# An opening reordered on five queues: GpSimd takes the subtraction for S4, the two weight groups of block 0 are split ahead of S3 and S4, and Bd's table is loaded earlier

## The reference

```
x = x + einsum('bct,bcd->bdt', x, W0[subject])
x = x + einsum('bct,bcd->bdt', x, W1[adapter])
x = x + einsum('bct,bcd->bdt', x, W2[adapter]) + fside[adapter][:, :, None]
gate = x @ Wg + (x @ Ag[adapter]) @ Bg[adapter]     # 512 -> 2048
up   = x @ Wu + (x @ Au[adapter]) @ Bu[adapter]     # 512 -> 2048
h    = silu(gate) * up
x = x + h @ Wd + (h @ Ad[adapter]) @ Bd[adapter]    # 2048 -> 512
```

## Time and profile before

| | us |
|---|---|
| median of 3 runs | 1249.04 |
| lowest, highest | 1248.89, 1249.17 |
| the profiled execution's own time | 1250.41 |
| its span, first to last instruction | 1248.4 |
| granted TensorE clock, mean | 1.000 |

### The profile page before, as it was taken

How to read it: one execution, slowest core, us unless ns; L and a number is a source line. 1 busy time by engine, 2 the same in 40 slices (tenths; PEclk the granted TensorE clock), 3 DMA queues, 4 the chain that set the end, 5 groups by cost and what they waited for, 6 DMA issues and landing times.

```text
span 1248.4 us, 17946 instructions
## 1 busy us (share of the span) xinstructions
PE 1236.3 (99%) x6222; PEld 1035.2 (83%) x6222; DVE 957.7 (77%) x1536; ACT 551.7 (44%) x987; POOL 710.7 (57%) x597
## 2 busy tenths in 40 slices
PE   8999999999999999999999999999999999999998
PEld 6888888888888888888888888888888888888887
DVE  6987777887778777788678768777867877677775
ACT  3744454444444354454334444444433443443432
POOL 4476556558745556546864556555676554444453
PEclk9999999999999999999999999999999999999999
DMA  5956455544896345445398535535559742323433
GB/s 186 308 193 212 119 143 147 160 137 136 310 316 216 107 129 147 129 145 171 119 373 297 168 101 152 152 120 155 146 186 359 251 118 78 95 82 102 118 87 116
DMA packets 142199, 211.68 MB, mean 170 GB/s; under 512 B 44192, under 2 KB 88480, under 8 KB 142112
## 3 DMA queue, kind: packets, MB, share of 16 engines
q1 hardware_dynamic: 117696, 135.45, 34.1%
q0 software_dynamic: 23552, 73.95, 19.2%
q10 hardware_dynamic: 864, 1.15, 0.3%
HBM read 166.46 MB, written 44.04 MB: 169 GB/s over the span
## 4 chain that ended last, share of the span: by engine, by line
PE 93%; DVE 4%; DMA 1%; issue 1%; ACT 1%; another core or an unknown queue 0%; SPq 0%; DVEq 0%; ACTq 0%
PE pd L1680 28%; PE px L1680 28%; PE py L1680 14%; PE pz L1680 7%; PE pz L1697 3%; PE pv L1726 2%; PE pv L1724 2%; PE pd L1986 2%; PE py L1697 2%; PE px L1697 2%; PE pd L1823 1%; PE pd L1707 1%; PE py L1805 1%; PE px L1805 0%; DVE wg_lo L1325 0%
## 5 line engine op out<-in xcount | busy, mean ns | idle before, releaser
L758 POOL TENSOR_TENSOR h_lo<-g,h_hi 128x512 fp32r<-128x512 f32 x127 | 182.8, 1439 | 288.0 <-ACT h_hi L898 285.6
L722 POOL DMA_INDIRECT b_got<-b_table,idx_b x192 | 197.8, 1030 | 59.0 <-issue 49.7
L1457 DVE TENSOR_TENSOR acc<-pd,acc 128x512 f32<-128x512 f32 x252 | 167.3, 684 | 55.1 <-PE pd L1680 50.9
L1680 PE MATMUL px<-xo_hi,wg_hi 128*128 128x512 f32 x516 | 207.2, 402 | 1.9 <-ACT up L898 0.6
L1325 DVE TENSOR_TENSOR wg_lo<-w_raw,wg_hi 128x512 fp32r<-128x512 f32 (+1 forms) x256 | 182.2, 716 | 32.7 <-issue 19.7
L1680 PE MATMUL pd<-wd_hi,h_hi 128*128 128x512 f32 x512 | 202.8, 396 | 0.0
L1680 PE MATMUL px<-xo_hi,wg_lo 128*128 128x512 f32 x516 | 202.4, 392 | 0.0
L1680 PE MATMUL pd<-wd_lo,h_hi 128*128 128x512 f32 x512 | 201.0, 393 | 0.0
L1680 PE MATMUL px<-xo_lo,wg_hi 128*128 128x512 f32 x516 | 200.9, 389 | 0.0
L1680 PE MATMUL pd<-wd_hi,h_lo 128*128 128x512 f32 x512 | 199.8, 390 | 0.0
L898 ACT ACTIVATE wg_hi<-w_raw 128x512 fp32r<-128x512 f32 (+1 forms) x260 | 146.3, 570 | 117.1 <-PE py L1697 73.9
(11 more groups left out here) (317 smaller groups left out, 2439.2 us busy)
## 6 DMA issues: line engine op xcount, KB each, us to landing
w_raw<-w_gu SPq DMA_DIRECT2D x65, 512.0 KB
wd_raw<-w_dn SPq DMA_DIRECT2D x64, 256.0 KB
xo_hi<-xops SPq DMA_DIRECT2D x21, 512.0 KB, 6.1
xo_lo<-xops SPq DMA_DIRECT2D x21, 512.0 KB, 7.4
acc<-x SPq DMA_DIRECT2D x8, 1024.0 KB, 8.7
ad_raw<-ad_table SPq DMA_DIRECT2D x16, 512.0 KB
xops<-st_hi SPq DMA_DIRECT2D x24, 256.0 KB, 2.8
xops<-st_lo SPq DMA_DIRECT2D x24, 256.0 KB, 2.9
```

Source lines behind the costliest of these rows:

```text
L722: gp.indirect_dma_start(out=dst, out_offset=None, in_=rows_of, in_offset=bass.IndirectOffsetOnAxis(ap=rows.bitcast(U32), axis=0)).then_inc ...
L758: return gp.tensor_tensor(dst, src_raw, src_hi, ALU.subtract)
L1457: ins = dve.tensor_tensor(dst, pd[j][:, :], dst, ALU.add)
L1680: ins = pe.matmul(psum, w_parts[wi], x_parts[xi], start=(start and i == 0), stop=(stop and i == 2), skip_group_check=more)
```

## The change

On five queues instructions are moved; none is added, and one changes its engine.

- SP: the load of `bd_rows` goes ahead of `store_ad(0, 0)`, `store_b(0)` and `load_b(1)`.
- POOL: Bd's subtraction comes after two of three gathers instead of after `b_low(1)`; the subtraction for S4 is POOL's now, after the six gathers of `b_got` and ahead of `gather_ad(0, 1..3)`.
- ACT: Bd's copy goes ahead of `b_high(1)`; the four `weights_high(1, g)` and the last two `ua_high` go ahead of `sum_high(S3)` and `sum_high(S4)`, with `keep_s1(1)` between; `weights_high(2, 1)` goes behind `keep_c21`; in block 1 of each quarter the second `down_high` goes behind `keep_s2`.
- DVE: `weights_low(1, 2)` and `(1, 3)` go ahead of `ua_low(0, 1, 0)`, `o_low(S3)` ahead of `select(0, 0)`, `o_low(S4)` is gone; in block 0 of the first quarter `select` and `c12` come ahead of `sums(2)` and `weights_low(2, 0)`; `half_numbers` goes from the start of block 1 to its end, ahead of `add_down`.
- PE: in block 0 of the first quarter `lora(pz, b, 0, 0)` comes after `S3` instead of before it.

```diff
@@ SP @@
             load_weights(1)
+            sp.wait_ge(pick_mm, 2)
+            sp.dma_start(bd_raw()[0], bd_rows).then_inc(bd_in, 16)
             store_ad(0, 0)
             store_b(0)
             load_b(1)
-            sp.wait_ge(pick_mm, 2)
-            sp.dma_start(bd_raw()[0], bd_rows).then_inc(bd_in, 16)
             load_ad(0, 0)
@@ POOL @@
-            gather_b(0, 0, 0)
-            b_low(1)
+            gather_b(0, 0, 0, range(2))
             gp.wait_ge(bd_hi_done, 1)
             low(bd_raw()[2], bd_raw()[0], bd_raw()[1]).then_inc(bd_done, 1)
+            b_low(1)
+            gather_b(0, 0, 0, range(2, CHUNKS))
             gather_b(0, 0, 1)
             gp.wait_ge(o_done, LOW_ORDER.index(S1) + 1)
             gp.wait_ge(o_s3_sum, TP)
+            gp.wait_ge(o_hi, HIGH_ORDER.index(S4) + 1)
+            gp.wait_ge(o_done, LOW_ORDER.index(S3) + 1)
+            low(xo_lo[:, S4, :], s_raw[S4], xo_hi[:, S4, :]).then_inc(o_done, 1)
             for g in range(1, AD_GROUPS):
                 gather_ad(0, g)
@@ ACT @@
             ua_high(0, 0, 1)
-            b_high(1)
             act.wait_ge(bd_in, 16)
             copy(bd_raw()[1], bd_raw()[0]).then_inc(bd_hi_done, 1)
-            sum_high(S3, o_s3_sum)
-            sum_high(S4, o_s4_sum)
+            b_high(1)
...
             ua_high(0, 1, 1)
+            keep_s1(1)
+            sum_high(S3, o_s3_sum)
+            sum_high(S4, o_s4_sum)
...
-                if b != 1:
+                if b != 1 and n > 1:
                     keep_s1(k)
...
                 keep_s5(k)
-                if b == 1:
-                    down_high(q * BLOCKS + 1)
...
                 keep_s2(k)
+                if b == 1:
+                    down_high(q * BLOCKS + 1)
...
                 if n == 1:
                     weights_high(n + 1, 0)
-                    weights_high(n + 1, 1)
...
                 if (q, b) == (0, 0):
                     keep_c21()
+                    weights_high(n + 1, 1)
@@ DVE @@
             o_low(S2, s_raw[S2])
-            ua_low(0, 1, 0)
             weights_low(1, 2)
             weights_low(1, 3)
+            ua_low(0, 1, 0)
+            o_low(S3, s_raw[S3])
             select(0, 0)
-            o_low(S3, s_raw[S3])
             ua_low(0, 1, 1)
-            o_low(S4, s_raw[S4])
...
                     u3(k)
+                    select(q, 1)
+                    c12(k)
                     if not q:
                         sums(n + 1)
-                    select(q, 1)
-                    if not q:
                         weights_low(n + 1, 0)
-                    c12(k)
...
-                if n == 2:
-                    half_numbers()
...
+                if n == 2:
+                    half_numbers()
                 for phase_at in down_phases(q, b):
@@ PE @@
                 product(pz, A12, True, True)
-                ... lora(pz, b, 0, 0).then_inc(p2_mm, 1)
+                if n > 1:
+                    lora11()
...
                 product(px, S3, False, True).then_inc(p7_mm, 1)
+                if n == 1:
+                    lora11()
```

More of the change, by code:

```diff
@@ L1972, in _, with lora11 @@
                 product(pz, A12, True, True)
-                pe.wait_ge(b_got_in[0], (q * SUPER + b // 2 + 1) * CHUNKS * 16)
-                pe.wait_ge(u_done, 6 * q + 3)
-                lora(pz, b, 0, 0).then_inc(p2_mm, 1)
+                def lora11():
+                    pe.wait_ge(b_got_in[0], (q * SUPER + b // 2 + 1) * CHUNKS * 16)
+                    pe.wait_ge(u_done, 6 * q + 3)
+                    lora(pz, b, 0, 0).then_inc(p2_mm, 1)
+                if n > 1:
+                    lora11()
                 pe.wait_ge(w_done[2], n + 1)
```

## The result

| | before | changed |
|---|---|---|
| median of 15 executions, us | 1249.17 | 1251.58 |
| lowest, highest | 1247.80, 1250.83 | 1249.19, 1256.61 |
| the profiled execution, own time | 1250.41 | 1251.75 |
| its span | 1248.4 | 1249.7 |
| granted TensorE clock, mean | 1.000 | 0.998 |

The account below looks back on a forecast made before the run. PE's own work was taken to set the time, leaving only its few pauses to gain. A gain of 1.9 us less 0.3 for `half_numbers` gave -1.6: median 1249.04 to 1247.4 us, range 1246.2 to 1249.2.

Parts of the forecast that it names:

- opening and block 0: Block 0: S3 starts at 49.62 on PE, S4 at 52.8; POOL's S4 subtraction takes 2.39 us and costs nothing.
- new wait for group 0 ahead of block 1: Block 1's start: PE waits 0.75 us for DVE's group 0, so A11 starts at 57.45, a gain of 0.75.
- block 1: Block 1 on PE: S3 at 63.4, a gain of 1.3 us; A22 at 66.85, a gain of 1.9.
- SP and the transfers: SP's queue: last store 62.3, `load_b(3)` 63.1, rows land 67.1; free up to 67.7, each us beyond costs one.
- Rival 3: Late gathers of Ad hold SP, then ACT in block 1: landing at 68.7 costs 1.0 us, 1248.3; chance 0.13.
- rival 5: Same SP queue with a transfer jam: rows for `b_high(3)` land at 72.1, 1251.6 us or more; chance 0.08.
- `half_numbers`: DVE, block 1's end: takes 1.6 us, 2.9 with one block; block 2 stalls 0 to 0.6, taken as 0.3.

Follow-up runs that it names:

- a0: The changed kernel again, unedited, on another chip: 1248.50 us against 1246.69 for the kernel before, ratio 1.0015.
- e1: Changed kernel with the first two gathers of Ad back ahead of S4's subtraction on POOL: 1254.39 us against 1252.92 before, ratio 1.0004.
- e7: Changed kernel with S4's subtraction back on DVE, behind the last `ua_low`: 1247.03 us against 1246.69 before, ratio 1.0000.
- e3: Changed kernel with the third store of Ad's rows moved on SP behind block 0's loads: 1250.94 us against 1252.92 before, ratio 0.9990.
- e4: Kernel before, with only its gathers of Ad made to wait for DVE's S4: 1255.23 us against 1252.92 before, ratio 1.0022.
- f3: Kernel before, with `half_numbers` alone moved from block 1's start to its end: 1249.65 us against 1248.92 before, ratio 1.0007.
- e2: Changed kernel with ACT's `b_high(3)` in block 1 moved behind the copies of block 2's weights: 1252.19 us against 1252.92 before, ratio 0.9995.
- f1: Changed kernel with SP's `load_b(3)` moved to the opening, right behind block 1's weights: 1248.56 us against 1248.92 before, ratio 1.0001.
- e6: e2 with `half_numbers` put back at the start of block 1: 1245.28 us against 1246.69 for the kernel before, ratio 0.9986.
- e8: e2 and e7 together, with `sums(2)` ahead of `select`, `c12` last, `half_numbers` at block 2's end: 1244.61 us against 1246.69 before, ratio 0.9985.
- g1: e8 with `select` ahead of `sums(2)` in block 0: 1248.28 us against 1249.61 for the kernel before, ratio 0.9990.
- f2: f1 with `sums(2)` ahead of `select`, `c12` last, `half_numbers` at block 2's end; S4 on POOL: 1247.49 us against 1248.92 before, ratio 0.9990.

## Why the prediction was wrong

**Held: opening and block 0.** POOL's subtraction took 2.42 us (2.39 forecast) and cost nothing. S3 and S4 started 5.49 and 8.74 behind block 0's A11 (49.62 and 52.8 less 44.12 are 5.50 and 8.68). The new wait for group 0 ahead of block 1 is 0.79 (0.75 forecast); A11 of block 1 gains 0.60 for 0.75.

**Held, a little small: block 1.** S3 gained 1.04 of 1.3, A22 1.58 of the 1.9.

**Failed: "SP and the transfers".** The step had the last store at 62.3, `load_b(3)` at 63.1, 4.0 us to land, 67.1, within the 67.7 that cost nothing. On this execution's scale, 0.61 less, the issue and the landing are 62.5 and 66.5; they were 64.15 and 69.66. So 1.6 us lay in the queue and 1.5 in the landing (5.5 us instead of 4.0). The queue's part is at the upper bound that the step gave (63.9 for the store and so 64.7 for the load, 64.1 on this scale). It also varies between executions: in a0 the issue came 19.0 us behind block 0's A11, just as the step had it. The term that fails in every profile is the landing, 4.0 us without any bound. It was taken from the one row of before. Where the load follows the stores in the changed kernel or an edit of it and ACT waits for it, it took 5.2 to 6.3 us (e1 5.2, first profile 5.5, e7 5.7, a0 5.8, e3 6.3), in e4 5.1, and even in f3, the kernel before with its transfers unmoved, 4.6. The DMA share from issue to landing was 0.82 in the kernel before, 0.94 in the first profile and 1.00 or more in the others. The rest of the step held roughly, each us beyond the free limit costing one: the landing exceeded the limit (67.1 on this scale) by 2.6 us and PE lost 2.19; in a0 it was 1.2 and 0.88. Rival 3 is this mechanism with the old landing time, and rival 5 its slower end; together they had 0.21. e4 shows the mechanism alone, e2 and f1 show that without it the loss ahead of `down` is gone. (The step counts 5.9 us from 47.67 to 53.75, which are 6.08; that changes nothing.)

**Not in the forecast at all: the clock.** 1.58 us of the loss in the profiled execution come from 1.2 GHz behind the pause; a0 has none of it and is still slower than before (ratio 1.0015). The executions without a profile fit this, though they don't prove it: of 15 of the changed kernel only one has a mean granted clock of 1.000; six at 0.999 have a median of 1250.5, seven at 0.998 one of 1252.3.

**Failed: `half_numbers`.** 0.3 us were taken, 0.6 as the bound of the likely case. Its length was nearly right, 3.2 us beside one POOL subtraction (2.9 forecast), 1.65 beside none in e2 (1.6 forecast). What was off is the time at which DVE comes to it: the step reckoned with 73.6 to 74.8, which is 29.5 to 30.7 behind block 0's A11, and a free DVE ahead. It was 33.8 in the first profile, 32.4 in a0, 32.7 in e2 and 33.0 in f1, since DVE was held by the late SiLU or, without that, by block 2's weights (1.08 us) and a gate product of 2.19 beside POOL. Where `down` paused for less than 0.8 us or not at all, block 2 lost 1.0 to 1.8 (a0, e1, e2, e3, e7, f1); with `half_numbers` elsewhere it lost nothing (e6, e8, g1) or 0.65, with the weights at their latest (f2).

**What the old place was worth.** `half_numbers` at the start of block 1 held `c11` until 67.31, and the rows for `b_high(3)` landed at 66.53. The old pause covered that landing. f3 takes it away alone: 0.54 us are gained, ACT waits 2.48 us for the rows but `down` isn't held yet, and block 2 loses 0.53. So of the two chains behind the pause the one over `half_numbers` had no room left, and the one over the rows had little.

By the sum: -1.58 (gain), +2.19 (pause), +1.58 (clock), +0.07, +0.17 (block 2) are +2.43 us at block 2's A22, against -1.6 forecast. That the medians differ by nearly the same, 2.41, is partly chance: the last matmul is 1.94 later, this execution reached block 0 0.61 earlier, and the two profiled executions' own times differ by 1.34; in a0 block 2's A22 is 1.12 later and the median 1.81.

**Open.** Why the rows took 5.5 us here, 6.3 in e3 and 4.0 before: the transfers queued around them differ, but no run changed these alone. What makes SP's queue late in the changed kernel other than the gathers' start (the earlier loads of Bd's rows and of the weights were never put back), and why it is 1.6 us later in one execution of it than in another. Why the clock falls behind some pauses and not others (below). On the chip of e1 to e4 PE pauses 1.4 to 2.2 us at the starts of two or three later quarters, in kernels that share this code with the others, whose profiles show no pause over 0.9 there; this is why the places there are compared only up to block 2.

## What to carry to other kernels

A pause on PE that is taken away uncovers what it covered: before a gain is booked, look which transfers land and which engines catch up during it. When a gather is moved later, follow the queue that stores it down to the last load behind, and price the landing of that load with a range of its own (4.0 to 6.3 us here for the same 256 KB), not with one row. Moving the consumer (ACT's copy behind its hidden values, e2) took the wait away as surely as moving the load (f1), and needs no transfer to be earlier. And profile the same kernel twice before a change of 1 us in a transfer's time is put down to an edit: two profiles of the changed kernel differ by 1.4 us in this landing.

## What the runs showed of the hardware

**The clock behind a pause.** PE's timeline and the windows behind it, of e3 and then of e1, later in the run:

```profile
348.99 0.53 PE L1833 MATMUL pd<-st_hi,v 128*128 128x512 f32 x1 [2.12 <-DVE acc L1467]
```

```profile
348.90:350.00 1.10, 1.01 (x3) 0.87 (x4) 1.06 (x4) 0.86 (x2) 0.00 (x0) 0.69 1.02 402
350.00:352.00 2.00, 2.00 (x6) 1.52 (x6) 2.00 (x4) 0.63 (x1) 0.00 (x0) 0.50 0.68 268
```

```profile
654.53 0.50 PE L1832 MATMUL pd<-st_hi,v 128*128 128x512 f32 x1 [2.17 <-DVE acc L1466]
```

```profile
654.50:657.00 2.50, 2.46 (x13) 2.13 (x14) 2.46 (x6) 1.44 (x3) 0.09 (x1) 1.00 0.77 305
```

After 2.12 us without a matmul the level fell to 1.2 GHz, after 2.17 it stayed at 2.4. It also fell after 2.04 in the changed kernel and after 2.13 in e2, and in the opening after 2.09 in e6 and 1.77 in e4 (granted clock 0.50 from 22 to 24 us), and not after 1.27 and 1.79 later in e4. So a pause of about 2 us can cost 1.6 us more than itself, but need not, and its length alone doesn't tell. In 34 executions of the kernel before on one chip the median time is 1251.5 us at a mean clock of 1.000, 1252.5 at 0.999, 1253.8 at 0.998 and 1255.3 at 0.997: about 1.3 us for each thousandth. On the chip of a0 the first step isn't there: 1246.69 in 23 executions at 1.000, 1246.52 in 11 at 0.999.

**One port pair.** A DVE gate product of 512 columns took 0.69 us with POOL idle (changed kernel, 70.85) and 2.19 beside a POOL subtraction of 1.31 (e2, 72.43 and 72.76), and a group of four instructions of 2 columns 0.38 beside none (e2, 75.12) and 1.89 beside one of 1.29 (changed kernel, 77.50 and 77.85). DVE's products that read one operand from a bank kept their 0.69 beside POOL's subtractions (changed kernel, `c11` at 63.12 and `u3` at 64.71, POOL busy from 62.28 to 67.32). The Trainium skill ("SBUF — State Buffer", section "SBUF: two separate sides") describes an exclusive lock on one pair of ports, held for a whole instruction, between GpSimd and those DVE instructions that have two inputs in SBUF or run in a two-port mode. These rows agree, with 1.50 and 1.51 us added where POOL's subtraction is 1.3 long. The section also says that whichever starts first gets the pair; in e2 DVE's row starts 0.33 us ahead of POOL's and is still the long one, so by the starts as recorded that isn't seen.
